# Two key-and-decay products moved ahead of the inverse assembly in a gated delta rule kernel

## What is computed

```python
mixed = silu(causal_conv1d(xn @ w_qkv, conv_w))          # 4 taps
q, k, v = split(mixed)                                   # q, k: l2 norm, each used by 2 value heads
beta = sigmoid(xn @ w_b);  g = -exp(A_log) * softplus(xn @ w_a + dt_bias)
def step(St, (q_t, k_t, v_t, g_t, b_t)):                 # 256 steps for each batch and value head
    St = St * exp(g_t)
    delta = (v_t - k_t @ St) * b_t
    St = St + outer(k_t, delta)
    return St, q_t @ St
core = rmsnorm(scan(step)) * norm_weight * silu(xn @ w_z)
out = x + core @ w_out + moe(xn)
```

## Time and profile before

| what | value |
|---|---|
| median of 3 runs | 1453.08 us (1449.57 to 1456.15) |
| span of the profiled execution, first to last instruction | 1450.2 us |
| TensorE busy | 1303.2 us, 90% |
| VectorE busy | 1055.2 us, 73% |
| ScalarE busy | 706.5 us, 49% |
| GpSimd busy | 650.4 us, 45% |
| mean granted TensorE clock | 0.958 of full |
| start of LA1 in iterations 0, 1, 14 and 15 | 477.7, 539.3, 1341.6 and 1400.0 us |

### The profile page before, as it was taken

One profiled execution on the slowest core, in us unless ns is written; L12 is line 12 of the kernel. 1 busy time (PEld: TensorE's weight loads), 2 busy tenths in 40 slices (PEclk: granted clock), 3 DMA queues, 4 the chain that ended last, 5 costly groups with the idle time before them and its releaser, 6 DMA issues.

```text
span 1450.2 us, 29334 instructions
## 1 busy us (share of the span) xinstructions
PE 1303.2 (90%) x10040; PEld 1092.1 (75%) x10040; DVE 1055.2 (73%) x1948; ACT 706.5 (49%) x1241; POOL 650.4 (45%) x1041
## 2 busy tenths in 40 slices
PE   6789999999857989989899999989999899999958
PEld 4678888888635868778687887868778687787846
DVE  2975555555477798888979888897888888879424
ACT  3434333342226656556565655655655565565411
POOL 2122222221118366383754738366384654836430
PEclk9999999999979999999999999999999999999858
DMA  5111111100220303213030230303213031230101
GB/s 212 44 44 45 43 43 43 49 0 0 74 72 14 98 16 92 46 63 107 15 94 19 89 92 24 99 16 93 53 55 107 17 92 34 74 85 15 27 16 37
DMA packets 100815, 81.81 MB, mean 56 GB/s; under 512 B 86832, under 2 KB 89904, under 8 KB 97360
## 3 DMA queue, kind: packets, MB, share of 16 engines
q1 hardware_dynamic: 100688, 80.11, 18.5%
HBM read 68.36 MB, written 11.73 MB: 55 GB/s over the span
## 4 chain that ended last, share of the span: by engine, by line
PE 27%; DVE 19%; POOL 11%; issue 6%; DMA 4%; ACT 3%; SPq 1%; POOLq 0%; DVEq 0%; ACTq 0%
POOL halves L812 6%; DVE conv L944 5%; POOL halves L809 5%; DVE eg L955 4%; DVE nm L976 4%; PE rv L1194 4%; PE ra L1159 3%; PE pj L1055 3%; PE pj L1057 2%; PE pj L1056 2%; PE pk L1093 2%; PE ra L1141 2%; PE ra L1149 2%; DMA r_scratch<-halves 1%; PE rv L1167 1%
## 5 line engine op out<-in xcount | busy, mean ns | idle before, releaser
L944 DVE SCALAR_TENSOR_TENSOR conv<-pj,taps,conv 128x510 f32<-128x510 f32 (+2 forms) x384 | 284.6, 745 | 60.7 <-ACT conv L841 50.2
L812 POOL TENSOR_TENSOR halves<-halves 64x30 f32<-64x30 f32 (+14 forms) x480 | 262.6, 547 | 37.7
L809 POOL TENSOR_TENSOR halves<-halves 64x30 f32<-64x30 f32 (+14 forms) x480 | 249.2, 519 | 37.6
L1055 PE MATMUL pj<-xhi,whi 128*128 128x512 f32 x384 | 168.8, 440 | 14.9 <-DVE conv L944 13.0
L1194 PE MATMUL rv<-wo,gated 128*128 128x256 f32 x512 | 144.5, 410 | 31.7 <-DVE f L1019 30.0
L233 POOL TENSOR_TENSOR w1lo<-w,w1hi 128x2048 fp32r<-128x2048 f32 x10 | 46.0, 4604 | 256.5 <-ACT w2hi L253 256.5
L1057 PE MATMUL pj<-xhi,wlo 128*128 128x512 f32 x384 | 151.5, 394 | 0.0
L1056 PE MATMUL pj<-xlo,whi 128*128 128x512 f32 x384 | 150.6, 392 | 0.0
L955 DVE TENSOR_TENSOR_SCAN eg<-eg,start 128x384 f32<-128x384 f32 x128 | 135.8, 1101 | 13.6 <-issue 12.1
L803 POOL MEMSET halves<- 64x32 f32 x16 | 2.4, 150 | 314.4 <-DMA halves<-n_scratch 314.3
L976 DVE SCALAR_TENSOR_TENSOR nm<-pk,wneg,eg 128x512 f32<-128x512 f32 (+1 forms) x256 | 140.3, 611 | 3.4
(11 more groups left out here) (161 smaller groups left out, 3080.1 us busy)
## 6 DMA issues: line engine op xcount, KB each, us to landing
eg<-eg_scratch SPq DMA_DIRECT2D x16, 1536.0 KB, 7.7
wraw<-w_heads SPq DMA_DIRECT2D x16, 776.0 KB, 6.4
w<-w_up SPq DMA_DIRECT2D x10, 1024.0 KB, 4.8
n_scratch<-nm SPq DMA_DIRECT2D x64, 96.0 KB, 2.6
w<-w_down SPq DMA_DIRECT2D x10, 512.0 KB, 5.6
wo<-w_out SPq DMA_DIRECT2D x16, 256.0 KB, 4.9
halves<-n_scratch SPq DMA_DIRECT2D x32, 128.0 KB, 2.5
r_scratch<-halves SPq DMA_DIRECT2D x32, 128.0 KB
```

Source lines behind the costliest of these rows:

```text
L809: gp.tensor_tensor(tmp, rb[:, 0:t, t:t + 1].to_broadcast([4 * NM, t, w]), rb[:, t:t + 1, t + 1:].to_broadcast([4 * NM, t, w]), ALU.mult).t ...
L812: gp.tensor_tensor(rb[:, 0:t, t + 1:], rb[:, 0:t, t + 1:], tmp, ALU.add).then_inc(elim, 1)
L944: v.scalar_tensor_tensor(out=y, in0=pj[j % 2][:, :, 0:S - s], scalar=taps[par][:, piece(j)[0], KS - 1 - s:KS - s], in1=y, op0=ALU.mult, op ...
L1055: te.matmul(bank, whi[par][w], xhi[:, k, cols], start=(k == 0), stop=False)
```

## The change

Two of the tables are rewritten; nothing is added or taken away. In ORDER, K2 and K3 now stand ahead of LA1, each further forward than before; TR1, TR2 and TR3 go in front of K2, and OUT0 and OUT1 behind it, P7 between them. In ORDER_V, K2 goes in front of OUT0, K3 in front of OUT2 and LA1. ORDER_A is as before.

```diff
-            ORDER = ("K0 P4 P5 SA TR0 K1 SO P6 OUT0 OUT1 K2 TR1 TR2 TR3 P7 OUT2 P8 OUT3 P9 P10 OUT4 P11 LA1 K3 LA2 P0 P1 "
+            ORDER = ("K0 P4 P5 SA TR0 K1 SO P6 TR1 TR2 TR3 K2 OUT0 P7 OUT1 K3 P8 OUT2 OUT3 P9 P10 OUT4 P11 LA1 LA2 P0 P1 "
...
-            ORDER_V = ("K0 P4 K1 SO P5 P6 OUT0 OUT1 P7 OUT2 K2 LA1 K3 P0 OUT3 OUT4 OUT5 OUT6 OUT7 SQ N21_0 N21_1 P1 P2 O0 O1 "
+            ORDER_V = ("K0 P4 K1 SO P5 P6 K2 OUT0 P7 OUT1 K3 OUT2 LA1 P0 OUT3 OUT4 OUT5 OUT6 OUT7 SQ N21_0 N21_1 P1 P2 O0 O1 "
```

## The result

The changed kernel takes 1547.88 us (median of 4 runs, 1538.68 to 1550.57) against 1454.62 us (1449.57 to 1456.83, 4 runs) for the kernel before on the same chip: ratio 1.0645, 95% interval 1.0606 to 1.0683. It is 93 us slower. The forecast was 1523 us, with a range of 1486 to 1556.

What follows compares the result with a forecast made beforehand. No single engine was taken as the bound: the elimination's circle (61.1 of 61.7 us) and the engines' order (61.3) share it. 5.3 + 0.85 - 0.4 = 5.75 us an iteration, 13 x 5.75 + 0.5 - 4.9 = +70, gave 1523 us, range 1486 to 1556.

Steps and rivals of the forecast that it cites:

- VectorE's queue: K1's end to LA1's transposes: K3 adds 4.84 us, the 1.72 us pause goes; 3.1 us lost without TensorE's share.
- OUT4's wait for OUT2: TensorE at OUT4 waits for OUT2, now behind K3 on VectorE; LA1 starts 2.42 us after OUT2 ends.
- The gap between LA1 and LA2: On TensorE, emptied of K3's products: P0 starts 3.6 us after LA1, 4.05 before, saving only 0.4 us.
- The clock: A clock fall behind OUT4's wait slows P11, LA1 and LA2 by 0 to 1.7 us an iteration; half taken, +0.85.
- Two of the signs I had named: LA1 every 67 us if the forecast is right; granted clock under 0.93 on the whole if the third rival is.
- the third rival: Much slower: TensorE's clock falls twice more on the path each iteration (3.4 us), +108 us or 1561; chance 12%.
- the upper bound of the sum: Whole loop: at most 7.0 us an iteration, +88 us in all, or 1541 us.
- GpSimd beside VectorE: K1's scans on VectorE meet only the elimination's small last steps; gain up to 0.8 us an iteration, 0.4 taken.
- TR3's wait: TensorE stands at TR3 from about 830.4 to 833.9 for ScalarE's copy of TR1; said to cost nothing by itself.
- The elimination: Its circle from K3's end to the next, 61.1 of 61.7 us; taking off 2.7 us of rf waits counted as 0.
- The faster case: The elimination is the true bound and K3 fits into 4.84 us of VectorE slack ahead of LA1; 1445.5 us, chance 6%.
- TensorE's wait for OUT2 and VectorE's K3 would lie in spare time: No change: both lie in time that the back half has to spare; 1453 us, chance 4%.

Runs made afterwards that it cites:

- out2_first: The changed kernel with OUT2 in front of K3 in VectorE's table, nothing else; 1518.4 us, ratio 1.0402 to the kernel before.
- p10_twice: The changed kernel with P10's 6 products made twice by TensorE, right ahead of the wait at OUT4; 1534.5 us, ratio 1.0564 to the kernel before.
- p0_in_gap: The changed kernel with P0 between LA1 and LA2 in TensorE's table; 1507.3 us, ratio 1.0356 to the kernel before.
- tr_early: The kernel before with TR1, TR2 and TR3 moved in front of OUT0 in TensorE's table, nothing else; 1470.3 us, ratio 1.0132.
- after_tr_late: The changed kernel with OUT0 in front of K2 and TR1 to TR3 behind K2 in TensorE's table; 1533.7 us, ratio 1.0541 to the kernel before.
- k3_only: The kernel before with K3 alone moved in front of LA1 in TensorE's and VectorE's tables; 1518.5 us, ratio 1.0419.
- tr_fill: The kernel before with TR1 and TR2 between OUT0 and OUT1 in TensorE's table, TR3 behind K2; 1452.9 us, ratio 0.9997.
- before_short: The kernel before with the elimination making only its last 14 of 30 steps, part of the inverse left out; 1394.4 us, ratio 0.9582.

## Why the prediction was right, and where its sizes were off

**VectorE's queue.** Forecast 14.77 + 4.84 = 19.61 us from K1's end to the end of OUT2; measured 19.65 to the transposes. The addend was right. What it replaced was not 16.49 but 16.08 us on average: the two neighbouring iterations that I read both had the pause of 1.7 us, and four of 13 do not have it. Those four follow the loop's boundary, where K1 ends 2 us later behind P0 (43.2 us instead of 41.2) and P7 is ready in time. The changed kernel has no pause that could absorb this. The cost was +3.57, not +3.12.

**OUT4's wait for OUT2.** Forecast +2.3 us from the transposes to LA1 on TensorE, with a wait of 2.1; measured +2.82, with a wait of 1.88 us. out2_first returned 30 us, where this term alone would give 13 x 2.3 = 30, in part by chance as said there. Part of the difference is again the choice of iteration: LA1 was usually 0.4 us ahead of the transposes before, not behind.

**The gap between LA1 and LA2.** Forecast 3.6 us from LA1 to P0, 0.4 less than before. At full clock it was 3.64 to 3.72 us, as in iterations 12 and 13. In the loop it was about 4.3, since LA2 ran at the slow clock.

**The clock.** This is the step that was mis-sized. "I take the half, +0.85" assumed at most one fall on the path, and argued that the wait at OUT4 is shorter than the one seen before. The trace shows a slow stretch of 7 us, not 4, behind LA1 in the iteration read. Over the loop window the granted clock is 0.92 where it was 0.98, another 0.06 x 800 = 48 us of full-speed clock gone in 11.6 iterations, about 4 us an iteration, of which part lies under other engines' work. What was on the path can be read by setting the loop against iterations 12 and 13, which ran at full clock behind LA1: LA1 to P0 is 4.25 us on average against 3.64 to 3.72, and P0 to K1's end 42.0 us, where no loop boundary lies between, against 40.1 and 39.8. That is about 2.6 us an iteration, an estimate; the forecast had allowed 0.85. The reason given for the half, that the wait at OUT4 is shorter than the one before (2.57 us), is refuted by p10_twice (a gap of 1.88 us) and p0_in_gap (1.35 us), each of which took the slow stretch behind LA1 away in most iterations or in all. The Trainium skill, "TensorE: Matmul & The Clock Gate", section "Why this matters for your kernels", warns of long idle gaps between bursts of matmuls. The fall behind the 3.35 us at TR3 agrees with it; the falls behind 1.88 and 1.35 us are not covered by it, and here the measurement decides. Two of the signs I had named show the same: LA1 comes every 69 us, not 67, and the mean clock of 0.924 lies under the 0.93 that I had set as the mark of the third rival. The measured time lies 25 us above the forecast and 13 under that rival's 1561, so the result is the forecast mechanism with a good part of the third rival in it. It also lies above the 1541 that I had worked out as the upper bound of the sum. The end of the range, 1556, was said to be half way towards the third rival, and it is not: half way from 1541 to 1561 is 1551, from 1523 it is 1542. The measured 1548 lies within the first and outside the second, so that it fell into the range owes something to where I drew its end.

Put together, the forecast was 5.3 us for the queues, 0.85 for the clock and -0.4 for GpSimd, 5.75 in all. Measured are 6.1 for the queues at full clock, about 2.6 and -1.2, or 7.5, against 7.44 in the table. The two errors of the small terms partly cancel.

**GpSimd beside VectorE.** Forecast a gain of 0.4 us an iteration. In iterations 12 and 13, which ran at full clock, P0 to K1's end is 40.1 and 39.8 us instead of 41.3 and 41.1, a gain of 1.2. The direction was right and the size three times larger.

**TR3's wait.** "This costs nothing by itself" was wrong for the TR items alone: tr_early costs 17 us, 1.3%, by a longer pause ahead of P7. The changed kernel has no such pause. Moving the wait there (after_tr_late) gave 14 us, with another gap in its place, so its own share in the changed kernel stays open.

**The elimination.** "In the middle of the loop only 2.7 us hang on rf" was read rightly, and its conclusion, that the engines alone need 61.3 us, was wrong: without most of the elimination they need 59.1 (57.8 and 60.4 in turn). What did hold is that an early K3 cannot turn this into time, since it puts 4.84 us into VectorE's queue. Waits for rf came only in the last group, 4.7 us on TensorE and 5.8 on VectorE, where I had said 2 to 3. Counted as the forecast counts, from P0 of iteration 13 to the last group's LA1 on TensorE, the end gave 5.4 us back, where I had said 4.9, and iteration 0 took 0.4 us less, where I had said 0.5 more. The whole miss lies in the 13 iterations between: counted from P0 each is 7.7 us longer, since this way iteration 1 is among them, where K2's scans met the split (3.6 us).

**The rivals.** The faster case needed 4.84 us of slack on VectorE ahead of LA1; there was 1.2 on average (16.08 less 14.87). That TensorE's wait for OUT2 and VectorE's K3 would lie in spare time is excluded by out2_first and by k3_only.

## What to carry to other kernels

With hand-written orders for engines that wait for each other, moving a producer earlier helps only if its queue has that much slack at the new place; count it over many iterations, not over one, because a pause need not come in each (here in nine of 13). Then ask what stood at the old place: K3's products filled a gap of TensorE's, and leaving it empty cost up to 41 us of 1548. Two halves of a change need not add up: where one has already made an engine late, the other finds slack. An item moved on one engine also changes which instruction of a third engine runs beside it: in tr_fill the scans moved under GpSimd's split and took back what the pause had given.

## What the runs showed of the hardware

- Two scans of VectorE that take 1.79 us alone took 4.87 us beside one GpSimd instruction of 3.48 us, whose end they waited out. This fits the rule that the two exclude each other for a whole instruction when VectorE has two inputs from SBUF and GpSimd's instruction reads SBUF, as the split does (the Trainium skill, "SBUF — State Buffer", section "SBUF: two separate sides"). The chained adds of P5 and P6, which read PSUM and one tile of SBUF, took 4.52 us beside the same GpSimd instruction in the changed kernel, and 4.52 us in the kernel before, where it ran at another time.
- More work made the program faster: 6 products more in each iteration, ahead of a gap of 1.88 us, took 13 us off the median (0.8%, barely clear of the scatter), with the granted clock up from 0.92 to 0.96 in the profiled run.
- P0 moved into a gap of 1.35 us, with no work added (p0_in_gap), left the granted clock behind LA1 at 1.00 in 13 of 13 iterations, where it had been 0.68 to 0.70 in 11.
- A wait of at most 1.6 us at OUT1 left the granted clock at 1.00 through the whole loop of before_short; in the kernel before, nine of the eleven waits of 2.1 to 2.6 us there were followed by a fall to the 1.2 GHz level. The two kernels differ in more than this wait, so a limit cannot be read from them: in the changed kernel falls followed gaps of 1.88 and 1.35 us that stand close together.
